# A two-layer perceiver kernel: context given transposed, pairs of tiles and eight GpSimd additions in the first cross attention; normalising moved to ScalarE in the second

## What is computed

```python
qh = (q @ Wq.T + bq).reshape(B, T, 16, 8)       # layer 0, 16 heads of width 8
kh = (k @ Wk.T + bk) ...; vh = (v @ Wv.T + bv) ...
attn = softmax(where(safe, einsum('bhqd,bhkd->bhqk', qh, kh) * scale, -inf))
out = einsum('bhqk,bhkd->bhqd', attn, vh) ... @ Wo.T + bo
```

## Time and profile before

| what | value |
|---|---|
| median of 3 runs | 3080.18 us (3079.72 to 3081.09) |
| the profiled execution's own time | 3079.37 us |
| its span in the trace | 3077.6 us, mean granted clock of TensorE 0.962 |
| busy over the span | TensorE 92%, its weight loads 53%, VectorE 64%, GpSimd 62%, ScalarE 48% |
| DMA | 233 MB |

### The profile page before, as it was taken

The page is one execution under the profiler, slowest core; times in us unless marked ns, Lnnn a source line. Parts: engine busy times, 40 slices in busy tenths (PEclk is TensorE's granted clock), DMA queues, the critical chain, the costliest instruction groups (busy, mean ns, idle before and its releaser), DMA issues. The chain is left out here.

```text
span 3077.6 us, 66754 instructions
## 1 busy us (share of the span) xinstructions
PE 2819.4 (92%) x22718; PEld 1618.6 (53%) x22765; DVE 1978.6 (64%) x4504; ACT 1479.6 (48%) x2385; POOL 1906.0 (62%) x1278
## 2 busy tenths in 40 slices
PE   5799999999999978998899999999999997888789
PEld 2355555555555566775344444444444443777356
DVE  5477777777777744114667767767767744776653
ACT  3466666666666522333544444444444434223633
POOL 5487878787878721001488888888888872553500
PEclk8899999999999989998999999999999998999789
DMA  7655555555555210001000000000000000000300
GB/s 184 187 174 193 177 190 181 184 186 179 194 175 188 100 58 1 1 0 39 22 33 21 21 32 21 21 32 21 21 32 21 21 1 9 3 3 2 85 5 10
DMA packets 146463, 233.18 MB, mean 76 GB/s; under 512 B 16787, under 2 KB 85851, under 8 KB 146076
## 3 DMA queue, kind: packets, MB, share of 16 engines
q1 hardware_dynamic: 145180, 228.87, 22.7%
q10 hardware_dynamic: 1152, 2.49, 0.6%
HBM read 147.80 MB, written 83.52 MB: 75 GB/s over the span
## 5 line engine op out<-in xcount | busy, mean ns | idle before, releaser
L444 POOL TENSOR_TENSOR sb_a_acc<-sb_a_acc,sb_a_PT 128x1024 f32<-128x1024 f32 x252 | 596.7, 2368 | 36.6 <-ACT sb_a_PT L522 30.3
L522 ACT ACTIVATE sb_a_PT<-ps_a_SC 128x1024 f32<-128x1024 f32 (+1 forms) x416 | 425.8, 1023 | 315.3 <-PE ps_a_SC L794 291.7
L607 DVE TENSOR_REDUCE sb_a_mx<-ps_a_A 128x1 f32<-128x512 f32 x768 | 506.4, 685 | 97.0 <-PE ps_a_A L771 91.8
L1686 POOL TENSOR_TENSOR sb_a_acc<-sb_a_acc,sb_a_PT 128x512 f32<-128x512 f32 (+2 forms) x384 | 487.5, 1269 | 37.3 <-ACT sb_a_PT L1782 10.9
L1782 ACT ACTIVATE sb_a_PT<-ps_a_SC 128x1024 f32<-128x1024 f32 (+2 forms) x256 | 234.3, 915 | 563.0 <-PE ps_a_SC L2061 329.3
L1875 DVE TENSOR_REDUCE sb_a_mx<-ps_a_A 128x1 f32<-128x512 f32 x384 | 256.5, 679 | 280.1 <-PE ps_a_A L2036 240.1
L2080 PE MATMUL ps_a_PV<-sb_a_PT,sb_a_XN 128*128 128x512 f32 (+2 forms) x896 | 434.3, 601 | 2.2 <-ACT sb_a_PT L1782 0.7
L2061 PE MATMUL ps_a_SC<-sb_a_QX,sb_a_XT 128*128 128x512 f32 (+1 forms) x832 | 396.7, 596 | 0.1
L771 PE MATMUL ps_a_A<-sb_a_KS,sb_a_QS 97*128 97x512 bf16 x768 | 301.9, 394 | 30.6 <-issue 17.7
L794 PE MATMUL ps_a_SC<-sb_a_QS,sb_a_KS 105*128 105x128 bf16 (+1 forms) x3328 | 257.3, 220 | 13.4 <-DVE sb_a_QS L621 13.4
L805 PE MATMUL ps_a_PV<-sb_a_PT,sb_a_V 128*32 128x256 f32 (+1 forms) x3328 | 266.7, 392 | 0.4 <-issue 0.3
(11 more groups left out here) (516 smaller groups left out, 5265.3 us busy)
## 6 DMA issues: line engine op xcount, KB each, us to landing
sb_a_C<-in_ctx_dram SPq DMA_DIRECT2D x64, 768.0 KB
a_KD<-sb_a_K SPq DMA_DIRECT2D x192, 256.0 KB, 4.1
sb_a_KS<-a_KD SPq DMA_DIRECT2D x256, 192.0 KB
a_KD<-sb_a_K SPq DMA_DIRECT2D x192, 144.2 KB, 2.7
sb_a_KS<-a_KD SPq DMA_DIRECT2D x256, 108.2 KB
sb_a_QP<-a_QD ACTq DMA_DIRECT2D x6, 384.0 KB, 14.7
sb_a_up<-in_moe_up_dram SPq DMA_DIRECT2D x1, 2048.0 KB, 7.9
sb_a_dn<-in_moe_dn_dram SPq DMA_DIRECT2D x1, 2048.0 KB, 12.0
```

Of the source, the lines that this page charges most:

```text
L444: pool.tensor_tensor(acc[:, :], first[:, :], PT[slot(a, j)][:, :], ALU.add).then_inc(s["acc"], 1)
L522: act.activation(PT[slot(a, j)][0:n, :], SC[(a + j) % 2][0:n, :], ACT.Exp).then_inc(s["exp"], 1)
L607: v.tensor_reduce(mx[:, p, c:c + 1], A[u % 2][:, :], AXX, ALU.max).then_inc(s["am"], 1)
L1686: pool.tensor_tensor(acc[a][0:m, :], first, PT[u % 4][0:m, HQ * i:HQ * i + HQ], ALU.add).then_inc(s["acc"], 1)
```

## The change

1. **First cross attention, context.** The host hands over `ctx_T`, batches x 128 x 1601, and the four weights transposed side by side. One DMA per batch fills `CT`; `C`, `CR`, `turn`, `turned` and the four transposes of weights are gone.
2. **First cross attention, order.** The step has 7 groups of two tiles. The sums on GpSimd are those of tiles 0 to 9 but for tile 3: eight additions. Keys of b+3 (chunks 0, 1) and b+2 (2, 3) share a step; the scores of the next batch's tiles 0 and 1 come at the very end; `top` goes to bank `A[0]`; VectorE's final work stands last. On SyncE spill and stack alternate, and load(2,0) moves behind pieces(1).
3. **Norms** in four chunks of four tiles, in all stages; in three places TensorE takes chunks 2 and 3 behind its first other work.
4. **Weights ahead.** delta0 also loads the weights of the second cross attention (transposed by the host), delta1 those of ffn1 (`ffn1_w`); transposes, copies and reorderings there are gone.
5. **Second cross attention, normalising on ScalarE** (`normed`): 13 activations a batch, out = crs * x + nb, with nb = -mean * crs from GpSimd; chunks 1 to 3 of b+2 at u = 1, 3, 5, chunk 0 of b+3 at u = 7. VectorE's `moments(b+3)` stand between `top` and `topped`.

```diff
@@ stage_xattn0 @@
-    COUNT = (0, 2, 2, 2, 2, 3, 3, 3, 3, 3, 3, 0, 0)
+    NG = (NK + 1) // 2
+    COUNT = (3, 5, 5, 5, 5, 3, 0)
+    SUMS = (1, 2, 4, 5, 6, 7, 8, 9)
-        return (1, 3, 5, 7, 9) if isinstance(b, int) and b == B - 1 else tuple(range(1, PTILE))
+        return (1, 3, 5, 7, 9) if isinstance(b, int) and b == B - 1 else SUMS
             def load(b, a):
-                wait(sp, s["ct"], 4 * (b - 1))
-                sp.dma_start(C[a][:, :, :], d["ctx_1024"][dsl(b), 0:KF * P, :].rearrange("o (p j) d -> p (o j) d", p=P))\
-                  .then_inc(s[f"ld{a}"], 16)
-                sp.dma_start(CR[a][:, :], d["ctx_1024"][dsl(b), KF * P:S, :].rearrange("o p d -> p (o d)"))\
-                  .then_inc(s[f"ld{a}"], 16)
+                wait(sp, s["vp"], 4 * (b - 1))
+                sp.dma_start(CT[a][:, :], d["ctx_T"][dsl(b), :, :].rearrange("o d s -> d (o s)")).then_inc(s[f"ld{a}"], 16)
@@ TensorE @@
             def step(b, a, n1, n2, n3):
+                for g in range(NG):
+                    us = list(units(g)) if n1 else []
...
+                    if g == 0 and n2:
+                        keys(b + 2, a, 2)
+                    if g + 1 < NG:
+                        for j in pair(g + 1):
+                            if g > 0:
+                                maxima(1)
+                            scores(b, a, j)
+                        maxima(1)
+                    if g == 1 and n2:
+                        keys(b + 2, a, 3)
+                    if g == 2 and n2:
+                        values(b + 2, a, 0)
+                    if g in (4, 5) and n3:
+                        keys(b + 3, 1 - a, g - 4)
+                    if g > 0:
+                        maxima(1)
+                    if g == NG - 1 and n1:
+                        top(b + 1)
+                    for j in pair(g):
+                        products(b, a, j)
+                    maxima(len(us))
+                    if g == 3 and n2:
+                        values(b + 2, a, 1)
+                    if g == 5 and n2:
+                        values(b + 2, a, 2)
                 total(b)
                 if n2:
                     values(b + 2, a, 3)
+                if n1:
+                    for j in pair(0):
+                        scores(b + 1, 1 - a, j)
@@ VectorE @@
+                if n2:
+                    residue(b + 2, 2)
+                for g in range(NG):
+                    for i, u in enumerate(units(g) if n1 else ()):
+                        tops(b + 1, u)
+                        if i == 3 and g == 1 and n2:
+                            residue(b + 2, 3)
+                        if i == 3 and g == 4 and n3:
+                            residue(b + 3, 0)
                 if n1:
                     top(b + 1)
+                if n3:
+                    residue(b + 3, 1)
+                if n1:
                     topped(b + 1, 1 - a)
                 if n2:
                     expand(b + 2, a)
+                if old:
+                    final(b - 1)
+                    invert(b - 1)
@@ norm_pool @@
-    pool.wait_ge(s["mean"], NT + 1)
-    pool.tensor_tensor(k.rstd[:, :], k.rstd[:, :], k.half[:, 0:NT], ALU.pow).then_inc(s["rstd"], 1)
+    for c in range(NT // 4):
+        r = k.rstd[:, 4 * c:4 * c + 4]
+        pool.wait_ge(s["mean"], 5 * c + 5)
+        pool.tensor_tensor(r, r, k.half[:, 0:4], ALU.pow).then_inc(s["rstd"], 1)
@@ stage_xattn1, ScalarE @@
+            def normed(b, a, c):
+                wait(act, s["nb"], b + 1)
+                for j in range(4 * c, min(4 * c + 4, NK)):
+                    m = wcols(j)
+                    act.activation(C[a][0:m, j, :], C[a][0:m, j, :], ACT.Identity, bias=nb[a][0:m, j:j + 1], scale=crs[a][0:m, j:j + 1])\
+                       .then_inc(s["z"], 1)
...
+                    elif two and u in (1, 3, 5):
+                        normed(b + 2, a, (1, 3, 5).index(u) + 1)
...
+                    if three and u == 7:
+                        normed(b + 3, 1 - a, 0)
@@ stage_xattn1, VectorE @@
-                wait(v, s["cp"], b + 1)
...
-                v.tensor_scalar(C[a][0:m, j, :], C[a][0:m, j, :], cag[a][0:m, j, 0:1], crs[a][0:m, j:j + 1], ALU.subtract, ALU.mult)
                 if one:
-                    top(b + 1, 1 - a)
+                    top(b + 1)
                 if three:
-                    norm(b + 3, 1 - a)
+                    moments(b + 3, 1 - a)
+                if one:
+                    topped(b + 1, 1 - a)
```

More of the change, by code:

```diff
@@ L186, in norm_vector, with moments @@
     src, dst = src or k.x, dst or k.hn
[L187 to L196, removed]
+    def moments(c):
+        tiles = range(4 * c, 4 * c + 4)
+        for n in tiles:
+            v.bn_stats(k.st6[:, n, :], src[:, n, :]).then_inc(s["stats"], 1)
+        for n in tiles:
+            v.wait_ge(s["stats"], n + 1)
+            v.bn_aggr(k.mv[:, n, :], k.st6[:, n, :]).then_inc(s["mean"], 1)
+        v.wait_ge(s["mean"], 5 * c + 4)
+        r, var = k.rstd[:, 4 * c:4 * c + 4], k.mv[:, 4 * c:4 * c + 4, 1]
+        if twice:
+            v.tensor_scalar(r, var, 1.0 + LN_EPS, LN_EPS * LN_EPS, ALU.mult, ALU.add).then_inc(s["mean"], 1)
+        else:
+            v.tensor_scalar(r, var, LN_EPS, None, ALU.add).then_inc(s["mean"], 1)
@@ L197, in norm_vector, with scaled @@
+    def scaled(c):
+        v.wait_ge(s["rstd"], c + 1)
+        for n in range(4 * c, 4 * c + 4):
+            v.tensor_scalar(dst[:, n, :], src[:, n, :], k.mv[:, n, 0:1], k.rstd[:, n:n + 1], ALU.subtract, ALU.mult)\
+             .then_inc(s["norm"], 1)
+    moments(0)
+    moments(1)
+    scaled(0)
+    moments(2)
+    scaled(1)
+    moments(3)
     if meanwhile is not None:
         meanwhile()
[L199 to L202, removed]
+    scaled(2)
@@ L780, in top @@
                 wait(pe, s["m1"], b + 1)
[L781 to L784 removed]
+                pe.transpose(A[0][:, 0:P], mxm[:, :], k.ident[:, :]).then_inc(s["mt"], 1)
             def scores(b, a, j):
@@ L873, in _ @@
             top(0)
-            scores(0, 0, 0)
+            for j in pair(0):
+                scores(0, 0, j)
             values(1, 1, 3)
+            for c in range(2):
+                keys(2, 0, c)
             step(0, 0, True, True, True)
@@ L1782, in probs, with step @@
                 act.activation(PT[u % 4][0:m, 0:n], SC[u % 2][0:m, 0:n], ACT.Exp).then_inc(s["exp"], 1)
-            def step(b, a, pair, one, two):
+            def step(b, a, pair, one, two, three):
                 for u in range(NB):
@@ L1925, in step @@
                         moments(2, 0)
-                    if first and u == 3:
-                        norm(2, 0)
-                    if u == 4 and three:
-                        moments(b + 3, 1 - a)
                     if first and u == 4:
@@ L1951, in _ @@
                 moments(b, b)
-            for b in range(2):
-                norm(b, b)
             for u in range(NU):
                 tops(0, u)
-            top(0, 0)
+            top(0)
+            topped(0, 0)
             step(0, 0, 0, True, True)
```

435 lines of the change are left out of this document (193 added, 242 removed).

## The result

The changed kernel takes **3165.32 us** (median, 3163.65 to 3172.18), the kernel before 3080.43: a ratio of 1.028, 95% interval 1.0262 to 1.0298. It is slower by 85 us, where 45 us faster was forecast: the sign of the forecast was wrong.

The account below looks back on a forecast made before the run. Both cross attentions were taken as bound by TensorE's stream. The terms -32 +3 -1 -2 -8 -6 +9 -8 summed to -45, against 3079.37 us that is 3034; forecast range 3012 to 3055 (0.62), eight in ten 2978 to 3064.

Parts of the forecast that it names:

- First attention, steady: First cross attention's steady batches: 1.1 us a batch less, a period near 30.1, -32 us over 29 intervals.
- My bound for the steady step: First cross attention: TensorE holes from 1 us a batch (-82 us) to 3.8 us (nothing gained).
- the one rival on the slower side: Second attention: ScalarE's chunk at the batch's end is uncovered and delays the exponential; +113 for +9, 3138 us; chance 0.05.
- The term that I did give: First attention's new order: 2.2 us a batch of matmuls removed, holes 2.7 against 1.6, net -1.1.
- the holes that I found: First attention, TensorE: holes at third tile's scores, around residues and at four row maxima, 2.7 us a batch against 1.6.
- The transposes' -1.60: First attention: removing thirteen TensorE transposes of the context saves 1.60 us a batch; ScalarE's copies behind them cost nothing.
- The title's part: First attention: GpSimd is 2.6 us early, so removing its ninth addition gains nothing; tile 3's ones matmuls cost +0.46 a batch.
- Prologue: First attention's start: load(2,0) ahead of batch 1's spill adds 3 us, from -3 to +6.
- Second attention, start: Second attention's beginning: preloaded, transposed weights give -8 us; first contexts normalised on ScalarE give -6.
- Second attention, steady: Second attention's steady batches: normalising on ScalarE costs +0.3 us a batch, +9 in 29; bounds -0.7 and +1.3.
- The price of the move: Second attention: thirteen normalisations moved from VectorE, 0.473 us each, to ScalarE, 0.298 each, 3.9 a batch.
- Norms and ffn1: Norms in four chunks: delta0 and delta1 -1 us together, experts -2; ffn1 -5 and its last norm -3.

Follow-up runs that it names:

- e2: The changed kernel with SyncE issuing both spills ahead of both stacks, as the kernel before did: 3096.9 us, ratio 1.0045.
- e7: The kernel before with one edit, SyncE's order made spill, stack, spill, stack: 3149.7 us, ratio 1.0224.
- e6: The changed kernel with half of the stacks left out from batch 2 on, so half the heads are scored against old keys: 3038.0 us, ratio 0.9866.
- e9b: The changed kernel with both spills ahead of both stacks, key pieces made earlier on GpSimd and ScalarE, second attention's norm on VectorE: 3007.0 us, ratio 0.9763.
- e8: The changed kernel with the first attention's old order and nine additions, only its transposes removed, and second attention's norm on VectorE: 3046.3 us, ratio 0.989.
- e3: The changed kernel with nine additions on GpSimd again and no ones matmuls for tile 3: 3168.4 us, ratio 1.0277.
- e10: The changed kernel with half of the stacks left out and nine additions on GpSimd: 3092.9 us, ratio 1.0037.
- e4: The changed kernel with the second attention's context normalised on VectorE again, moments at u = 4: 3139.2 us, ratio 1.0181.
- e5: The changed kernel with the edits of e2 and e4 together: 3062.0 us, ratio 0.9951.
- e12: e9b with the second attention normalised on ScalarE, chunk 0's activations moved ahead of the copies at the batch's end: 2996.4 us, ratio 0.9726.
- e1: The changed kernel with the three bfloat16 key pieces held twice, by the batch's parity, no order changed: 3170.9 us, ratio 1.0282.

## Why the prediction was wrong

- **First attention, steady: the failed step is one that isn't in the sum.** I costed TensorE's and VectorE's new lists and wrote of SyncE's only in the prologue. That spill and stack now alternate in every step stood in the change's own description and had no term. What the runs showed in its place is a queue loop of 34.3 us with two waits of about 7 us for landings, where I had a period of 30.1; it came out at 33.95. e2 and e7 price the alternation at 70 us. And even without it the period is 31.35 (e2), as the new order makes the key pieces late; that had no term either. My bound for the steady step (from -82 to nothing) took in holes on TensorE alone, and the one rival on the slower side was another stage's.
- **The term that I did give was too small.** -1.1 a batch was forecast for the new order; with the queue out of the way (e6, e9b) it is 31.23 - 29.48 = 1.75. By TensorE's busy time, 30.4 us a batch before and 28.1 in e6, the removed work is 2.3, near my 2.2; the idle time grew by 0.6 where I had walked 1.1. So the holes that I found were about 0.5 too many. The period of 30.1 was near to what those two kernels do, not to the change; there, "wrong over 30.9", which I gave as the test, is what came.
- **The transposes' -1.60** was right for the new order's sum, but not as a price of its own: in the old order they cover reduces, and e8 gets 0.44. "The copies behind them were cover and cost nothing" looked at ScalarE; the cover that mattered was TensorE's own.
- **The title's part.** "Worth nothing by itself" held in the changed kernel (e3), "needed only as the period shrinks" held too (e10), but I took the slack from the end of GpSimd's list, 2.6 us, and it is consumed at the slots in the middle: 2.0 us a batch at 29.5.
- **Prologue**: +3 was forecast. The second `top` came at 129.2 us, before at 134.9. That is less certain than it looks: in the ten other kernels with the changed prologue it comes between 131.5 and 134.3, and in e7, with the old one, at 131.5. So neither +3 nor -5.7 is shown. The load among the spills does show: SyncE waited 17.1 us for the landing ahead of the second batch's first stack, where it had waited 7.2, but issued that stack in 8.2 us and not in 19.0, so from the spill to the stack's end it took 31.3 and before 31.1.
- **Second attention, start**: -8 and -6 forecast. The first batch's copy comes 103.0 us into the stage (before 110.6), -7.6 for both together. e4 parts them: with the first contexts normalised on VectorE again it comes at 100.1. So the preloading with the norm gave -10.5 for -8, and the move to ScalarE, for which I had -6, cost 2.9 (1.5 between e2 and e5, 1.8 between e9b and e12). The row maxima did come off VectorE's path, 9.4 us of TensorE's waits for VectorE in e4 against 3.7 in the change, but copies on ScalarE came late in their place (the change, TensorE's own waits, 1498 to 1602 us; in e4 the same wait is 1.7):

```profile
PE ps_a_SC L2026 <- ACT sb_a_QT L1759: 7.2, 3, 4.6
```

- **Second attention, steady: mis-sized.** +0.3 a batch forecast, +0.99 measured, inside the bound of +1.3. I had "0.9 to 1.3 late, part of it covered by products". It was 1.65 late, of which no part was covered, less the 0.67 that I had counted. The activations start at 1840.59 in the trace, behind all copies, and the transposes at 1842.37.
- **The price of the move was mis-sized too.** Four of the activations, in the changed kernel's timeline of ScalarE, and the exponential behind them:

```profile
1840.59 1.64 ACT L1799 ACTIVATE sb_a_C<-sb_a_C,sb_a_nb,sb_a_crs 128x128 f32<-128x128 f32 x4
...
1842.13 1.01 ACT L1815 ACTIVATE sb_a_PT<-ps_a_SC 128x1024 f32<-128x1024 f32 x1
```

From start to start that is 0.385 each, where I took 0.298 from the row of twenty, an activation whose scale is a column, too, but with no bias. Thirteen are 5.0 us a batch, not 3.9. The same work on VectorE before, in a steady step:

```profile
1862.72 4.94 DVE L1869 TENSOR_SCALAR sb_a_C<-sb_a_C,sb_a_cag,sb_a_crs 128x128 f32<-128x128 f32 x13
```

0.38 each: the move neither shortened the work, as I wrote from the earlier trace rows, a duration where starts should be compared, nor lengthened it. By the figures of the Trainium skill (VectorE: DVE Perf Modes, "The TRN2 errata") ScalarE would, by estimate, take 0.293 and VectorE 0.194. Both rows here are above them, VectorE's by a factor of two, and e12, with the move kept, is 11 us faster than e9b with the norm on VectorE.

- **Norms and ffn1** came near (experts -2.3 for -2). The -8.1 for -8 of ffn1 is partly luck: up to its last norm it is -6.9 for -5, behind it -1.2 for -3. A power of four columns takes 1.03 us where 1.0 to 1.3 was worked out. delta0 got 2.0 longer, not shorter. Seven more loads are issued there, but e7, which has none of them, shows the same 86.5 us, and e10, which has them, 83.6; the cause stays open.

## What to carry to other kernels

A queue that only issues is an engine too: write its loop down for one period, with each landing that it waits for, and compare the sum with the period: here 34.3 against 31.2. A transfer whose landing the queue itself waits for belongs ahead of the bulk transfers, not behind one; here that order was worth 70 us either way. And removed work is worth its time only where nothing waits in its place; price it with the neighbours that it kept apart.

## What the runs showed that I had not expected

- A wait taken away can come back whole in another row, at the same period (e1: 46.9 us of ScalarE's waits gone, 41.6 on TensorE instead). The row that stayed, SyncE's 173 and 177 us, was the cause.
- The granted clock went with the holes: from 260 to 760 us its mean was 0.94 in the change (period 33.95), 0.96 in e7, 0.98 in e2, and 1.00 in e6, e8 and e9b. TensorE is busy 30.0 us a batch in the change and 28.1 in e6, for the same matmuls. How much of the longer period comes from that, and how much is hidden in the queue's loop, wasn't told apart.
- DMA traffic at 185 GB/s was taken for a possible bound in several expectations. It moved 195 GB/s in e9b: the 185 had been what the schedule asked for.
- The gain of one GpSimd addition was 0, or 2.0 us a batch, by the bound of the kernel that it is in.
